# Attention and expert layer on one core: the second pass's scores signalled by the next slot's first pass, and a tile's turned queries and keys signalled once per pair of banks

## The reference

```python
        att = jnp.einsum('bhgqd,bhkd->bhgqk', q, k) / scale
        causal = jnp.tril(jnp.ones((t, t), dtype=bool))
        att = jnp.where(causal, att, jnp.asarray(-jnp.inf, att.dtype))
        att = jax.nn.softmax(att, axis=-1)
        y = jnp.einsum('bhgqk,bhkd->bhgqd', att, v)
        y = y.transpose(0, 3, 1, 2, 4).reshape(b, t, N_EMBD)
        return y @ Wo.T + bo
```

## Time and profile before

| | us |
|---|---|
| median of 3 runs | 1365.22 (1358.71 to 1370.29) |
| span of the profiled execution | 1391.8 |
| a beat with all its parts, 366.25 to 453.23 of the span | 86.98 |

### The profile page before, as it was taken

One profiled execution on the slowest core, in us unless ns is written; L12 is line 12 of the kernel. 1 busy time (PEld: TensorE's weight loads), 2 busy tenths in 40 slices (PEclk: granted clock), 3 DMA queues, 4 the chain that ended last, 5 costly groups with the idle time before them and its releaser, 6 DMA issues.

```text
span 1391.8 us, 24100 instructions
## 1 busy us (share of the span) xinstructions
PE 1093.7 (79%) x7305; PEld 840.2 (60%) x7305; DVE 708.7 (51%) x2229; ACT 663.5 (48%) x1650; POOL 717.7 (52%) x953
## 2 busy tenths in 40 slices
PE   3798998888888888889765058888878887888875
PEld 1566665565655655566534057777767777777773
DVE  3466776575666756666425411112245444545456
ACT  2466655555555555565331034444445444544451
POOL 3111125646557465474575745555555556555652
PEclk9599999999999999999867579899989999999987
DMA  2587886212122121122228865555768687766536
GB/s 83 171 277 228 265 264 230 103 35 100 60 70 101 35 102 61 50 100 64 90 89 293 269 192 158 167 160 169 232 216 288 228 281 233 278 218 232 182 124 206
DMA packets 142828, 233.22 MB, mean 168 GB/s; under 512 B 17303, under 2 KB 119910, under 8 KB 137840
## 3 DMA queue, kind: packets, MB, share of 16 engines
q1 hardware_dynamic: 67936, 101.06, 22.6%
q0 software_dynamic: 27600, 69.28, 13.9%
q10 hardware_dynamic: 47168, 61.35, 13.3%
HBM read 107.32 MB, written 132.53 MB: 172 GB/s over the span
## 4 chain that ended last, share of the span: by engine, by line
PE 50%; DVE 16%; another core or an unknown queue 13%; issue 10%; ACT 4%; POOL 3%; DMA 3%; ACTq 0%; DVEq 0%; SPq 0%; POOLq 0%
PE psB L1386 9%; PE psD L1403 7%; DVE nmax L866 6%; PE psv L601 4%; PE psA L1376 4%; PE ps L505 3%; PE psp L498 3%; PE psp L484 3%; PE ps L552 3%; PE psC L1394 3%; PE ps L512 2%; DMA x_d<-oT 2%; POOL rows_d L457 1%; PE psq L628 1%
## 5 line engine op out<-in xcount | busy, mean ns | idle before, releaser
L1467 POOL DMA_INDIRECT res_d<-y,dst_i x319 | 320.1, 1003 | 238.2 <-ACT y L1290 137.7
L866 DVE TENSOR_REDUCE nmax<-ps 128x1 f32<-128x512 f32 (+3 forms) x448 | 225.8, 530 | 138.7 <-PE ps L512 92.6
L457 POOL DMA_INDIRECT rows_d<-pay,slot_i x256 | 254.8, 996 | 74.2 <-issue 72.3
L732 ACT ACTIVATE wgu_s<-ps 128x512 f32<-128x512 f32 x320 | 191.6, 600 | 121.4 <-PE ps L512 92.4
L1191 DVE TENSOR_TENSOR inner<-inner,psB 128x128 f32<-128x128 f32 x160 | 45.9, 287 | 300.5 <-ACT inner L1277 206.2
L1386 PE MATMUL psB<-wgu_s,xT 128*128 x1276 | 183.9, 290 | 17.5 <-ACT xT L1270 11.2
L1403 PE MATMUL psD<-wdp_s,innerT 128*128 x638 | 177.5, 400 | 17.5 <-ACT innerT L1283 10.3
L1386 PEld LDWEIGHTS psB<-wgu_s,xT 128*128 128x128 f32 x1276 | 167.6, 205 | 22.2 <-issue 21.9
L505 PE MATMUL ps<-kT,qT 96*128 96x512 f32 (+3 forms) x512 | 168.0, 390 | 8.3 <-DVE nmax L866 5.5
L512 PE MATMUL ps<-mask,ident_b 128*128 128x256 bf16 (+1 forms) x640 | 174.3, 272 | 0.0
L552 PE MATMUL ps<-qT,kT 128*128 128x512 f32 (+3 forms) x512 | 164.0, 383 | 4.5 <-ACT wgu_s L732 3.9
(11 more groups left out here) (257 smaller groups left out, 1610.0 us busy)
## 6 DMA issues: line engine op xcount, KB each, us to landing
rows_d<-blank ACTq DMA_DIRECT2D x8, 5440.0 KB, 19.1
xg<-rows_d SPq DMA_DIRECT2D x160, 272.0 KB
yk<-res_d SPq DMA_DIRECT2D x28, 1024.0 KB
wgu_s<-wgu_in ACTq DMA_DIRECT2D x8, 1024.0 KB
x_d<-x SPq DMA_DIRECT2D x30, 192.5 KB
xs<-x_d SPq DMA_DIRECT2D x30, 192.5 KB, 3.3
res_d<-y,dst_i POOLq DMA_INDIRECT x319
wgu_s<-x_in SPq DMA_DIRECT2D x32, 128.0 KB, 2.2
```

The costliest lines, as they stand in the source:

```text
L457: pool.indirect_dma_start(rows_d, bass.IndirectOffsetOnAxis(ap=slot_i[par][:, t, k:k + 1], axis=0), pay[par][:, t, :], None).then_inc(s_sc ...
L732: act.activation(pexp[p % 4][:, s, :], ps2[:, (5 * p + s) % 2, :], ACT.Exp, scale=HEAD_D ** -0.5).then_inc(s_exp, 1)
L866: return dve.tensor_reduce(nmax[u][:, tile, heads[0]:heads[-1] + 1], src, AX.X, ALU.max, negate=True)
L1467: pool.indirect_dma_start(res_d, bass.IndirectOffsetOnAxis(ap=dst_i[:, j % (2 * G):j % (2 * G) + 1], axis=0), y[:, j % Y, :], None, bounds ...
```

## The change

Two signals of PE are thinned out, and the waits for them are rewritten. First, the masks of the second pass raise s_s2 only for the last nine slots of the whole attention (320 slots; `told`). For the 311 others, who wants second pass q waits for s_s1 to count q + 10: the first pass that PE issues in the next slot, after second pass q (BEHIND is 9). Second, the eight transposes of a tile's queries, and of its keys, raise s_split_ps once, after the eighth, where they raised it after the fourth and the eighth. ACT's first copy therefore waits for both banks, and the second for nothing more.

```diff
+            BEHIND = UNIT + 4
+            TOLD = BATCH * SLOTS - BEHIND
+
+            def wait_scores2(eng, q):
+
+                if q < TOLD:
+                    eng.wait_ge(s_s1, q + BEHIND + 1)
+                else:
+                    eng.wait_ge(s_s2, q - TOLD + 1)
...
-                            last.then_inc(s_split_ps, 1)
+                        last.then_inc(s_split_ps, 1)
...
+                def told(ins, q):
+
+                    if q >= TOLD:
+                        ins.then_inc(s_s2, 1)
...
-                        masked(ps2, bank, mask2, 0, 4).then_inc(s_s2, 1)
+                        told(masked(ps2, bank, mask2, 0, 4), 5 * U + s)
...
-                        act.wait_ge(s_split_ps, held(4 * tile))
+                        act.wait_ge(s_split_ps, 2 * tile)
...
+                        act.wait_ge(s_split_ps, 2 * tile + k - 8)
                         for half in range(2):
-                            act.wait_ge(s_split_ps, 4 * tile + 2 * (k - 9) + half + 1)
...
-                    act.wait_ge(s_s2, 5 * U + s + 1)
+                    wait_scores2(act, 5 * U + s)
```

More of the change, by code:

```diff
@@ L566, in pass2 @@
                         scoresT(h, par, p, bank, 384, 3, s - 2)
-                        masked(ps2, bank, mask2, 0, 3).then_inc(s_s2, 1)
+                        told(masked(ps2, bank, mask2, 0, 3), 5 * U + s)
                     else:
@@ L570, in pass2 @@
                         scoresT(h, par, p, bank, 256, 2, 1)
-                        masked(ps2, bank, mask2, 0, 2).then_inc(s_s2, 1)
+                        told(masked(ps2, bank, mask2, 0, 2), 5 * U + s)
                 def main(now, one, two, s):
@@ L712, in pre @@
                         if t == 0 and k == 9:
-                            act.wait_ge(s_s2, held(40 * (b - 1)))
+                            if b >= 2:
+                                wait_scores2(act, SLOTS * (b - 1) - 1)
                         rows = 96 if k == 9 else P
+                        act.wait_ge(s_split_ps, 2 * tile + k - 8)
                         for half in range(2):
-                            act.wait_ge(s_split_ps, 4 * tile + 2 * (k - 9) + half + 1)
                             act.copy((qT if k == 9 else kT)[par][0:rows, 4 * half:4 * half + 4, t * P:(t + 1) * P],
@@ L768, in post @@
                         act.wait_ge(s_pv, BATCH * KV_HEADS)
-                        act.wait_ge(s_s2, BATCH * SLOTS)
+                        wait_scores2(act, BATCH * SLOTS - 1)
                         part, width = (t - 2) * 6 + k, EXPERTS * KC * GU // (2 * TILES)
@@ L1158, in _ @@
                 dve.tensor_scalar(offs, owner[0:1, :], float(D), None, ALU.mult).then_inc(e_offs, 1)
-                dve.wait_ge(s_s2, BATCH * SLOTS)
+                dve.wait_ge(s_s2, BATCH * SLOTS - TOLD)
                 dve.memset(wdp_s[INNER:P, :], 0.0).then_inc(e_wdp_zero, 1)
```

## The result

The changed kernel takes 1435.41 us (median of 4 runs, 1427.87 to 1442.67) against 1366.66 for the kernel before: a ratio of 1.0522, interval 1.0483 to 1.0561. The forecast was 1363. The change costs 69 us where 2 were to be won; the time lies above the range, and the side is the one that had 0.26.

What follows compares the result with a forecast made beforehand. No engine is full; half the chain of waits is PE's work, with late PE signals stalling DVE in attention. 1391.8 - 21 + 19 = 1390 for the span, 2 us less, taken from the median: 1363 us, range 1335 to 1390.

Steps and rivals of the forecast that it cites:

- Loss 19 us, ends 0 and 38: Attention: exponentials start later, delaying the ACT copies behind them and so PE; 38 us, halved to 19.
- Half of it taken back: Attention: PE regains half of the 38 us, since its lateness is free where it waits for DVE anyway.
- The copies counted: Sixteen ACT copies a beat (normed tile, queries, two in `post`, four tiles); a third cost 1 us: 5 us a beat.
- Gain 21 us: Attention: fewer signals shorten DVE's waits for late PE signals, one 1.43 us step each; 21 us, ends -5 and 45.
- A signal costs PE's pace nothing: PE in attention: the 375 removed signals have zero price in a quiet place; up to 0.02 us each could hide.
- The rival of that name: Every signal costs PE time, at most 0.02 us for each of 375, 7.5 us: about 1355 us; chance 0.06.
- The rival of the vanished hold-ups: Attention: a third fewer PE signals stop late-signal delays from forming; 45 us back against 19 lost: 1339 us; chance 0.30.
- The rival in which PE waits for ACT: Attention: PE gets nothing back, loss 38 us, gain 15: 1388 us; sign, beats of 89 us or more; chance 0.22.
- The signs of being right: DVE's second-tile wait near 3.3 us, exponentials 0.3 to 1 us after masks, PE's three-line waits some 15 us.
- The first copy waits for four transposes more ... hides behind: ACT's first copy of a tile: 0.34 us later, covered by the later exponential in front; uncovered, 22 us of ACT's time.
- So I add nothing: Second pass q + 2 waits for exponential q; two PE passes between fit ACT's 0.60 us, so no loss.
- The sum's base: Profiled span lies 1.9% above the median; late-signal delays may be larger there than unprofiled, which would shrink the gain.

Runs made afterwards that it cites:

- the second profile: The kernel before, unchanged, profiled once more: span 1377.1 us, on a chip where its median is 1382.88 us.
- the turn: Kernel before, all signals in place, exponentials wait for the next slot's first pass only at 64 in front of turned queries' and keys' copies: 1413.16 us, 1.0324.
- The lateness alone: Exponentials wait for the next slot's first pass as in the changed kernel, but every second-pass and bank signal is raised: 1429.01 us, 1.0483 to the kernel before.
- the told kernel: The changed kernel with each turned bank signalled again, after the fourth and eighth transpose: 1431.29 us, 1.0474 to the kernel before.
- the kernel before in the new order: The kernel before, all signals in place, with ACT's exponential of a slot moved behind the next slot's steps of `pre`: 1386.91 us, 1.001.
- the single signal alone: The kernel before with only the single signal for a pair of turned banks; the second pass signals each slot: 1370.22 us, 1.0053.
- the reordered kernel: The changed kernel with ACT's exponential moved behind the next slot's steps of `pre`, except at the first tile's values: 1382.17 us, 1.0135 to the kernel before.
- the three groups of exponentials: Kernel before, all signals, late wait only before copies of: turned queries/keys (64), 1.0324; casts and values (64), 1.0078; the rest (112), 1.0039. All 240: 1.0587.

## Why the prediction was wrong

**The step that failed** is the term "Loss 19 us, ends 0 and 38". Its mechanism was the right one, an exponential that waits for the next first pass with PE's copies behind it on ACT. Its size was some 66 us: the lateness with all signals in place costs 4.83% of 1362. The term priced PE's waits at their own length and put what follows from them at nothing: that the same matmuls then take longer. The points of the working, one by one:

- *What follows a wait* had no term. In the attention PE's matmuls took 31.6 us longer (581.02 to 612.57), while its idle time, which is all that the term counts, grew by 15.1, or by 20.2 against the second profile. Part of this is the clock, which fell from 0.93 to 0.90 in the mean. As an estimate, the same kinds of matmul compared at the two levels within each trace put the cost of the lower level at 34 us in the attention before and at 56 in the changed one, so at some 22 of the 32. The two first beats with the same idle time point the same way: 71.55 us busy at 0.73, 67.41 at 0.80. What the other 10 us are is open, and no run holds the clock up while PE waits, so its share is not isolated by experiment.
- *Half of it taken back* held. What I took before halving, 5 us a beat, is what PE's waits for ACT grew by: 29.0 less 9.2 in four beats. Its idle time in these four beats grew by 1.9 us a beat (51.9 to 59.6 in all), where 2.5 were forecast. So more than half came back, 1.4 us a beat of it at the three lines for DVE (22.4 us, now 9.0, 5.3 and 2.7); some of the rest is the shorter hold-up of slot 19.
- *The copies counted* came out right in sum by luck. Of the two places worked out, the fourth tile's queries are there (PE waits for them in slot 36 for 3.0 us in five beats, 0.6 a beat in place of 0.8 to 0.9); the copy of a normed tile is not (0.7 us in four beats). I let all sixteen copies of a beat count alike and left those of the keys out. The runs show one kind that matters: the turn costs 44 us, in 28 turned tiles (four in each of the seven beats that prepare a sequence) 1.6 us a tile. There the queries' copy, PE's keys and the keys' copy follow one upon another, each copy behind an exponential of its own.

The idle time that the traces show does not fill up the 69 us of the medians: PE's 31.6 and 15.1 are 46.7, and 54.2 against the second profile. The first profiled execution of the kernel before lies 25 us over its median, so part of the loss is hidden in it; where the rest of the difference lies is open.

**Gain 21 us** was wrong as well, and here the mechanism. I took a signal that is not sent to save a step of 1.43 us in a hold-up. The lateness alone with all signals (1.0483) and the told kernel without 311 of them (1.0474) are equal within their intervals, and 1024 signals more change neither the time nor DVE's wait. The hold-up at the second tile's turn did shrink, by 2.6 us in the mean of five beats; but in the kernel with all signals and the late wait it shrank by 2.8. Fewer signals are therefore not needed for it. Nor is the lateness: with every signal and nothing late, the kernel before in the new order has 3.13 us there, and the one with the single signal alone, where nothing is late either, 3.64. Small moves of ACT's work seem to be enough, but what in them does it is open; that slot already differs by 1.1 us between the two profiles of the kernel before (5.80 and 4.68).

**A signal costs PE's pace nothing:** right, and firmly: at most 4.6 ns. The 26.3 ns of the Trainium skill (TensorE: Matmul & The Clock Gate, The cost: per-tile semaphore tail) would be 27 us for 1024 of them; the run shows no such price on each signal. That page gives it for a tail behind a group of tiles; these matmuls stand in a stream, and whether that is the difference no run here tests. The rival of that name falls with it.

**The rival of the vanished hold-ups**, 0.30, falls: twice the signals did not lengthen them, and where they did shrink, no time was won. (Its 2.9 us a beat for the second hold-up don't follow from the earlier trace rows, which add up to 2.2.) Nor did the rule of the Trainium skill on spacing increments (VectorE: DVE Perf Modes, The TRN2 errata) show in this kernel: twice as many of PE's signals did not delay anything; that rule speaks of several engines, and only PE's were added.

**The rival in which PE waits for ACT** came nearest. Beats are 89 us or more (91 to 96 for the five with scatters), and over the four beats PE waits for ACT for 29.9 us in all its lines, more than for DVE (24.2); for ACT's copies alone, as the sign was put, it is 22.9. Its premise, that PE gets nothing back, did not hold, and its price, 1388, was 47 us short for want of the same term.

**The signs of being right** were half met: PE's waits for the lines that were 717, 697 and 783 grew to 22.7 us (some 15 were named), and DVE's wait at the second tile's turn fell to 1.77 (3.3 was named). The sign of being wrong altogether was not met: the experts moved by 12.6 us, the attention by 49.

**"The first copy waits for four transposes more ... hides behind":** right in the changed kernel, where adding the single signal to the told exponentials moves the ratio by no more than the intervals (1.0474 and 1.0522). Where the cover is gone, as the exponential in front is not late or stands behind, it costs 0.5% (the single signal alone) and some 0.7% (1.0135 less 1.0068, in the reordered kernel); the bound of 22 us that I gave holds.

**"So I add nothing"** for the second pass two slots on: right, since 80 late exponentials with no copy behind them cost nothing.

**The sum's base.** I feared that the span, 1.9% above the median, holds hold-ups that other executions lack. Something of that kind: in the second profile the attention is 7.8 us shorter and the experts 7.0, so these belong to the execution and not to the kernel.

What stays open: about 0.7% that the reordered kernel still loses with each bank signalled; why the three groups of exponentials cost 1.5% more together than one by one, beyond that it comes in the beats with scatters; and what makes a hold-up, besides scatters close by.

## What to carry to other kernels

When a wait is moved to a later event, don't ask who needs its result; list what stands behind the waiting instruction on its engine, and find the first piece there for which the busiest engine waits. Where nothing of that kind stands there, lateness is free (1.0002 here), and where the late instruction can be moved behind it, most of the price goes (5.2% to 1.35%). Any idleness that this puts on PE should be priced with the matmuls that get slower after it (8.9 us for 4.2 in the first beat, 1.7 for 4.1 in the second, whose clock did not fall), and a signal should be priced by a run with twice as many before a change is made to save some.

## What the runs showed of the hardware

- A thousand signals more on TensorE's matmuls, about as many again as the attention has, cost 0.05% (-0.24 to 0.34).
- What waits for TensorE's masks started up to 3.7 us after their ends, in beats in which POOL's indirect DMAs run. The profile models the ends of matmuls, so it does not tell a late signal from a late end. Without DMAs in the slots around the place, VectorE's wait fell from 3.3 to 1.0 and 1.8 us; the kernels with the same DMAs moved elsewhere were slower by 4.0% and 1.3%.
- A beat without a hold-up in which TensorE idles 4.2 us more ran its 399 matmuls in 67.4 us in place of 58.5, at a granted clock of 0.80 for 0.89; another with the same idle time ran them in 71.6 us, at 0.73.
